# Half of a shared expert moved from the router's stage into the opening of the attention, in a one-core Flamingo stack

## The reference

```
x = x + tanh(g_xattn[0]) * quantised_expert(layernorm(x), ...)        # layer 1
x = x + tanh(g_ffn[0])   * ffn0(layernorm(x))                         # layer 2
x = x + tanh(g_xattn[1]) * attention(layernorm(x), ctx, pos)          # layer 3
x = x + tanh(g_ffn[1])   * ffn1(layernorm(x))                         # layer 4
```

```
scores = softmax(xt @ gate_w.T);  idx = top_k(scores + gate_b, 2)
y = sum over the 2 chosen experts of weight * (silu(xt @ W1[e].T) * (xt @ W3[e].T)) @ W2[e].T
z = (silu(xt @ Ws1.T) * (xt @ Ws3.T)) @ Ws2.T                         # shared expert, every token
return y + z
```

## Time and profile before

| | us |
|---|---|
| median of three runs | 1374.13 |
| the profiled execution | 1370.09 |
| its span | 1368.3 |
| TensorE busy | 1163.8 (85%) |
| VectorE busy | 826.9 (60%) |
| ScalarE busy | 672.5 (49%) |
| GpSimd busy | 404.8 (30%) |

### The profile page before, as it was taken

One profiled execution on the slowest core, in us unless ns is written; L12 is line 12 of the kernel. 1 busy time (PEld: TensorE's weight loads), 2 busy tenths in 40 slices (PEclk: granted clock), 3 DMA queues, 4 the chain that ended last, 5 costly groups with the idle time before them and its releaser, 6 DMA issues.

```text
span 1368.3 us, 16555 instructions
## 1 busy us (share of the span) xinstructions
PE 1163.8 (85%) x5247; PEld 510.3 (37%) x5309; DVE 826.9 (60%) x1275; ACT 672.5 (49%) x1191; POOL 404.8 (30%) x477
## 2 busy tenths in 40 slices
PE   5787786999699999953459989999999999888898
PEld 3454444555344444421013222222332222234443
DVE  6787855116055555215788888777877777613543
ACT  3565564545222222242347666566656556763453
POOL 5555720111222222113434432222222233102332
PEclk9998998999899999985669999999999999999999
DMA  7333135432434444337713332222222236200011
GB/s 253 116 108 108 58 120 182 162 127 92 158 123 147 150 144 147 100 129 216 192 51 106 90 103 73 81 86 79 71 88 78 83 84 67 37 1 8 32 39 47
DMA packets 110452, 141.58 MB, mean 103 GB/s; under 512 B 24888, under 2 KB 79672, under 8 KB 110376
## 3 DMA queue, kind: packets, MB, share of 16 engines
q1 hardware_dynamic: 91528, 111.37, 25.3%
q0 software_dynamic: 18368, 28.85, 8.3%
q10 hardware_dynamic: 480, 0.39, 0.1%
HBM read 97.44 MB, written 46.27 MB: 105 GB/s over the span
## 4 chain that ended last, share of the span: by engine, by line
PE 30%; DVE 9%; issue 8%; ACT 6%; POOL 2%; DMA 1%; POOLq 0%; ACTq 0%; DVEq 0%
PE PS L2717 8%; PE PS L2687 5%; PE PS L2631 5%; PE PS L2655 5%; ACT a_E L2798 4%; PE PS L2704 4%; DVE a_top L2975 4%; POOL a_K L2029 1%; DMA a_attnT<-f_y,l_pos 1%; PE PS L2258 1%; DVE a_tab L2055 1%; DVE a_early L2877 1%; PE PS L2281 1%; PE PS L2627 1%; PE PS L2648 0%
## 5 line engine op out<-in xcount | busy, mean ns | idle before, releaser
L2975 DVE TENSOR_REDUCE a_top<-PS 128x2 f32<-128x1024 f32 x256 | 308.3, 1222 | 94.1 <-PE PS L2704 89.9
L2798 ACT ACTIVATE a_E<-PS 128x512 f32<-128x512 f32 x512 | 277.7, 596 | 147.7 <-PE PS L2687 147.4
L2687 PE MATMUL PS<-a_Q,a_K 99*128 99x512 bf16 (+1 forms) x468 | 157.4, 387 | 17.5 <-ACT a_E L2798 7.6
L2704 PE MATMUL PS<-a_K,a_Q 64*128 64x512 bf16 x512 | 104.5, 405 | 45.9 <-DVE a_top L2975 26.9
L1464 PE MATMUL PS<-f_W,f_GT 128*128 x312 | 141.9, 598 | 0.0
L2717 PE MATMUL PS<-a_E,a_V 128*32 128x512 f32 x1024 | 139.0, 615 | 0.6 <-ACT a_E L2798 0.4
L2687 PEld LDWEIGHTS PS<-a_Q,a_K 99*128 99x128 bf16 (+1 forms) x512 | 44.4, 97 | 154.2 <-ACT a_E L2798 102.3
L1891 POOL TENSOR_TENSOR a_qf<-a_qf,a_tab 128x512 f32<-128x512 f32 x15 | 19.1, 1271 | 267.1 <-DVE a_swapped L2899 267.1
L1520 DVE TENSOR_TENSOR f_H<-f_SG,PS 128x256 f32<-128x256 f32 x39 | 16.4, 421 | 125.1 <-ACT f_SG L1504 125.1
L1464 PEld LDWEIGHTS PS<-f_W,f_GT 128*128 128x128 f32 x312 | 57.0, 193 | 57.4 <-issue 57.4
L2704 PEld LDWEIGHTS PS<-a_K,a_Q 64*128 64x128 bf16 x512 | 24.7, 93 | 139.2 <-issue 73.5
(11 more groups left out here) (362 smaller groups left out, 1987.7 us busy)
## 6 DMA issues: line engine op xcount, KB each, us to landing
f0r_raw<-in_L_ffn_W_dram SPq DMA_DIRECT2D x24, 512.0 KB, 4.9
a_K<-k_parts SPq DMA_DIRECT2D x192, 64.0 KB, 2.3
a_Q<-a_q_parts SPq DMA_DIRECT2D x186, 64.0 KB, 2.5
f_y<-f_Y SPq DMA_DIRECT2D x39, 256.0 KB, 2.0
v_units<-V SPq DMA_DIRECT2D x16, 512.0 KB, 2.9
a_V<-v_units SPq DMA_DIRECT2D x16, 512.0 KB, 3.6
k_parts<-f_k_parts SPq DMA_DIRECT2D x16, 384.0 KB, 3.5
a_q_parts<-a_parts SPq DMA_DIRECT2D x16, 384.0 KB, 2.7
```

The source lines that it names most:

```text
L2687: nc.tensor.matmul(PS[:, 4 + h % 2, :], K6[k][0:rows_, o, head // 2, kt * P:(kt + 1) * P], Q6[k][0:rows_, o, head // 2, :], start=True, st ...
L2704: last = nc.tensor.matmul(PS[:, 2 * pair + o, :], Q6[k][at, o, h // 2, t * P:(t + 1) * P], K6[k][at, o, h // 2, :], start=True, stop=True)
L2798: nc.scalar.activation(E[step % 2][:, h, :], PS[:, 4 + h % 2, :], ACT.Exp).then_inc(exp_done, 1)
L2975: nc.vector.tensor_reduce(top[:, h - h % 2:h - h % 2 + 2, t], PS[:, 2 * pair:2 * pair + 2, :], AX.X, ALU.max).then_inc(maxed, 1)
```

## The change

1. **The front runs the shared expert for eight tiles, not sixteen.** The batches are taken in the order 2, 0, 3, 1. For batches 0 and 1 the shared expert is computed as before, one tile with one expert's six fills (four behind the up product, two behind the transposes of H). Batches 2 and 3 only go through the router; ScalarE's queue stores their transposed rows to DRAM. The shared weights stay in SBUF, in a buffer that later serves as the exponentials' `E0` and as `attn`.
2. **The other eight tiles run in the attention's opening** (`LateTiles`). Two loads of 1 MB bring the transposed rows into `attnT0` and into `wo`; the first is SP's first transfer, the second takes the place of Wout's load, which waits for the last up product. VectorE makes the gate product and adds the result straight from PSUM. A table `LATE` says which step stands in which slot.
3. Rows of tiles 8 to 15 are added in turns (0, 0) to (0, 3), two tiles to a turn; the `fill`s of the constant rows stand at slots of a table; ScalarE's half of the first queries' load goes from the end of turn (-1, 1) to slot 3 of (-1, 2).
4. **In the last stage** batch 2 is normalised and batch 3's statistics are taken beside the last projections, in turn (4, 0); `choose` is cut in two around the second gate product.

```
         def front(first_set, turn, logit, tile, choose, count, place):
             turn(0)
             logit(0)
+            first_set()
+            turn(1)
+            tile(0, lambda: logit(1), None)
+            tile(1, None, None)
+            turn(2)
+            tile(2, lambda: logit(2), None)
+            turn(3)
...
+            tile(3, last_logits, None)
+            tile(4, None, count)
+            tile(5, None, None)
+            tile(6, None, place)
+            tile(7, None, None)
...
             def turn(n):                      # ScalarE
...
+                if TURNS[n] in LATE:
+                    act.wait_ge(xT_ready, (n + 1) * DC)
+                    act.dma_start(xT_late[TURNS[n] - LATE[0]], xT[BUFFER[n]][:]).then_inc(xT_stored, 16)
...
+            def tile(j, beside, behind):      # TensorE
+                for c in range(DC):
+                    last = nc.tensor.matmul(PS[:, 5, 0:2 * I], rows[:, c, at], shared13[:, c, :], start=(c == 0), stop=(c == DC - 1))
+                last.then_inc(up_done, 1)
+                if beside:
+                    beside()
+                for f in fills(j)[:DC]:
                     turned.tensor(pe, f)
+                if behind:
+                    behind()
                 if j:
                     down(j - 1)
                 pe.wait_ge(gated, j + 1)
...
                 last.then_inc(h_turned, 1)
+                for f in fills(j)[DC:]:
+                    turned.tensor(pe, f)
...
+class LateTiles:
+    DOWN = (6, 0, 1, 2, 6, 6, 6, 6)
...
+    def load(self, sp, k):
+        sp.dma_start(self.homes[k], self.xT_dram[k]).then_inc(self.loaded[k], 16)
+    def silu(self, act, n):
+        act.wait_ge(self.up_done, n + 1)
+        if n >= 2:
+            act.wait_ge(self.gated, n - 1)
+        self.nc.scalar.activation(self.SG[n % 2], self.bank(n)[:, 0:self.I], ACT.Silu).then_inc(self.silu_ready, 1)
+    def gate(self, v, n):
+        v.wait_ge(self.silu_ready, n + 1)
...
+        self.nc.vector.tensor_tensor(self.H[n % 2], self.SG[n % 2], self.bank(n)[:, self.I:2 * self.I], ALU.mult).then_inc(self.gated, 1)
+    def add(self, v, n):
+        v.wait_ge(self.down_done, n + 1)
+        x = self.X[:, self.first + n, :]
+        self.nc.vector.scalar_tensor_tensor(x, self.PS[:, self.DOWN[n], :], self.tgate, x, ALU.mult, ALU.add).then_inc(self.added, 1)
...
+        LATE = {(-1, 0): {9: [("g", 2, 0), ("y", 0, 0), ("y", 1, 0), ("t", 2, 0)]},
+                (-1, 2): {4: downs(2) + ups(3), 5: [("g", 3, 0), ("y", 2, 0)] + ups(4), 6: [("t", 3, 0), ("g", 4, 0)] + downs(3),
...
         def tiles_to_add(b, c):
-            if b == -1:
-                return [TB + 2 * c, TB + 2 * c + 1]
-            if b == 0:
-                return [3 * TB + c]
+            if b == -1 and c < 2 or b == 0:
+                first = TB + 2 * c if b == -1 else 2 * TB + 2 * c
+                return [first, first + 1]
             return []
...
                 def scores(unit, step, h):
-                    if not (is_first(unit) and step == 0 and h < 2):
+                    if is_first(unit) and step == 0 and h < 2:
+                        pe.wait_ge(late.HT_ready, late.N)
...
+            FILLS = {(-1, 0): {11: [(1, 0)], 12: [(1, 1)], 13: [(1, 2)]}, (-1, 1): {4: [(1, 3)]},
+                     (-1, 2): {3: [(2, 0), (2, 1)], 8: [(2, 2)], 9: [(2, 3)], 10: [(3, 0)], 11: [(3, 1)], 12: [(3, 2)], 14: [(3, 3)]}}
...
+                if b == NB:                   # VectorE
+                    def third_rows():
+                        v.wait_ge(x_added, 3 * TB)
+                        f1.statistics(v, 2)
...
+                    at(6, third_rows)
+                    at(8, third_normalized)
+                    for t in range(TB - 1):
+                        at(10 + 2 * t, lambda t=t: fourth_rows(t))
```

More of the change, by code:

```diff
@@ L815, in moe_front @@
-        LAST = NB - 1
-        def front(first_set, turn, logit, tile, choose, count, place, end):
+        shared13, shared2 = shared_weights(shared_w, I, D)
+        turned = Weights(nc, sb, sem, PS, identf, W13, W2, shared13, shared2, *raw)
+        SG = [sb(f"SG{k}", [P, I]) for k in range(2)]
+        UP = [sb(f"UP{k}", [P, I]) for k in range(2)]
+        H = [sb(f"H{k}", [P, I]) for k in range(2)]
+        HT = [sb(f"HT{k}", [P, IC, P]) for k in range(2)]
+        Z = [sb(f"Z{k}", [P, D]) for k in range(TB)]
@@ new lines, in moe_front, with fills, fills_in_front, front @@
+        up_done, silu_ready, gated, h_turned = sem("up_done"), sem("silu_ready"), sem("gated"), sem("h_turned")
+        HT_ready, down_done, z_ready, added = sem("HT_ready"), sem("down_done"), sem("z_ready"), sem("added")
+        FILLS = Weights.FILLS
+        assert E == NS
+        def fills(j):
+            return range(FILLS * (j + 1), FILLS * (j + 2))
+        def fills_in_front(n):
+            return FILLS * (0, 1, 3, 4)[n]
+        def front(first_set, turn, logit, tile, choose, count, place):
@@ L2698, in maxima @@
                             pe.wait_ge(ones_ready, 4 * (k + 1))
-                    if not (is_first(unit) and h == 0):
+                    if is_first(unit) and h == 0:
+                        pe.wait_ge(late.added, 3 + pair)
+                    else:
                         pe.wait_ge(maxed, n_max(unit, h, pair) - 2)
@@ L2836, in _, with add_rows @@
             rows.vector_start(v)
-            for t in range(TB):
+            rows.vector(v, 0)
+            late.gate(v, 0)
+            rows.vector(v, 1)
+            late.gate(v, 1)
+            rows.vector(v, 2)
+            rows.vector(v, 3)
+            def add_rows(t):
+                if t >= late.first:
+                    v.wait_ge(late.added, t - late.first + 1)
                 rows.vector(v, t)
@@ L2946, in outs @@
                                                            ALU.mult, ALU.add).then_inc(x_added, 1)
+                    for kind, m, part in late_jobs(b, c, n):
+                        if kind == "g":
+                            late.gate(v, m)
+                        if kind == "y":
+                            late.add(v, m)
                 if (b, c) == (NB - 1, 2):
```

480 lines of the change are left out of this document (290 added, 190 removed).

## The result

The changed kernel takes 1333.62 us (median of 4 runs, 1332.65 to 1335.91) against 1372.93 (4 runs) of the kernel before: a ratio of 0.9708, with a 95% interval of 0.9691 to 0.9725. In two later comparisons it was 0.9698 (0.9679 to 0.9717) and 0.9714 (0.9695 to 0.9733). 1328.5 was forecast, 1318 to 1346 as range. The profiled execution took 1335.91 us, the longest of the first four, with a span of 1334.1 us: 34.2 less than before, where the medians differ by 39.3.

What follows compares the result with a forecast made beforehand. TensorE bounds the front and leads the body; gathers, a chain and VectorE bound the opening in turn. -39 + 1.5 + 3 - 8.5 = -43.0 from 1370.09 gives 1327.1, plus 1.4 for the median: 1328.5, range 1318 to 1346.

Steps and rivals of the forecast that it cites:

- The front, -39: Front of layer 2: eight tiles less give 43.0 us, less 1.6 and 2 of waits; -39, between -43 and -34.
- the bound of 3.0: Front, tile 1: largest wait for raw W1/W3, landing after at most 9.2 us and needed after 6.2.
- The second rival: Front becomes bound by raw weight loads: seven tiles wait 3.0 us each, +19, 1347 us; chance 0.08.
- To the first transposes, +1.5: Opening's start: 1 MB more at the head of SP's queue delays the gathers; +1.5 us.
- The strict reading, +3.9: Opening's start: the added 1 MB load ahead of the gathers is paid in full, +3.9 us instead of +1.5.
- Clock and queries, -1.5: Opening: late tiles keep the clock up; transposes gain, queries' gain is lost to fills on ScalarE; -1.5 us (0 to -3).
- The queries' load, +2: Opening: ScalarE's half is issued later, behind second unit's queries and two fills; tiles 3 and 4 included; +2 us (0 to +4).
- The maxima, -1.5: Opening, VectorE-bound: four row pairs leave (-6.0), gates and adds come (+3.5), +1 for TensorE-led slots; -1.5 us (-2.5 to +12).
- First unit +1, body +3: First unit: down product, add and Exp table at its head, +1 (0 to +4). Body: four more waits behind adds, +3.
- The last stage, -8.5: Last stage: earlier statistics shorten two waits for xT and keep the clock; -8.5 us, between -11 and -5.
- The third rival: Opening gets shorter: gathers lose nothing, VectorE's gain comes through, clock stays up; -6 instead of +1.5, 1321 us; chance 0.10.
- The first rival: Opening can't take the tiles: clock stays low in the maxima; +18 instead of +1.5, 1345 us; chance 0.15.

Runs made afterwards that it cites:

- the four edits: Changed kernel with third store later, first units' K and V loads behind the gathers, third silu behind square root, batch 1's normalising behind seventh gate: 1319.8 us, 0.9619.

## Why the prediction was right, step by step

- **The front, -39: held,** -37.5 in the profile. Eight tiles less is as reckoned, the turns wait 0.97 us each instead of 0.8, and the router costs nothing. The mis-sized term is tile 1's load, 2 forecast, 3.42 of waiting and 1.5 of low clock measured (in the other profiles mostly 2.6 and 1.4). The store was named as what disturbs it, and moving it gives 3.6 us of the front back. But the bound of 3.0 had a mistake in it. It counted 6.2 us from request to need, with a down product of 1.7 us between. Tile 0 has no tile before it and so no down product: the loads are issued at 248.28 and needed at 252.77, 4.5 us later. They land after 7.9, inside the 9.2 of the earlier trace rows, from which the bound should have been 4.7, with the fall of the clock on top. The second rival (every tile late) did not come: tiles 2 to 7 wait for no weights.
- **To the first transposes, +1.5: right within the scatter,** and not shown closer than that: +1.2, +1.2, +1.4, +1.6, +2.7, +3.6 and +4.2 in seven profiles, against a single one of before. The strict reading, +3.9 for the megabyte ahead, falls: the same megabyte once more cost 0 and 1.2 us. What the gathers pay for is the K and V loads beside them (with the second half of the turned rows behind these), and K and V stood there before the change too. That queues share the DMA engines, as the Trainium skill says (Trainium Kernel Development and Optimization, Key Constraints), agrees with the 4 us that leave with those loads; it doesn't give the price of a load ahead.
- **Clock and queries, -1.5: wrong.** Transposes still at 1.11 and queries of 5.9 to 6.6 us (5.38 before) made it +0.5 to +1.2. The forecast had the late tiles shortly ahead of them; they end 5 to 8 us earlier, and the clock falls in between. Where they end 0.8 us earlier, it holds (0.66 and 3.67).
- **The queries' load, +2, and tiles 3 and 4:** with the item above the stretch from transposes to maxima grew by 0.4 to 1.1 (forecast +0.5).
- **The maxima, -1.5: the step that failed,** +3.2 to +4.7. Three things are in it. First, the forecast took four row pairs off this stretch (6 us), but only three stood in it; in the kernel before, the fourth is added behind TensorE's first scores (704.26):
```profile
704.71 0.74 DVE L1577 SCALAR_TENSOR_TENSOR X<-a_rows,a_tw,X 128x512 f32<-128x512 f32 x1
```
Three pairs are 4.5 us, and without late tiles the stretch is 3.2 shorter (42.0 to 38.8). Second, of the tiles' price 6.5 was measured instead of 4.5. VectorE's busy time went from 41.0 to 41.6 us, where three pairs less and 3.5 us of late tiles more would be 40.0, and its idle time grew from 1.1 to 3.7 us. Third, and part of that, late tiles have a fixed order against VectorE's other work: the seventh gate stands behind a normalising of 2.28 us, and TensorE waits 3.47 us for it. The move behind the gate brings the maxima to 44.0 and 43.5 us, so 1.3 us or more hang on it; what the rest is, no run shows.
- **First unit +1, body +3: less than forecast,** -0.2 and +1.2, and undoing the move won nothing in the body. VectorE's idle time takes most of the extra adds: nearer to the lower bound of 0 than to the 0.75 us behind each.
- **The last stage, -8.5: held.** It lasts 110.4 us where before had 120.7, and undone it costs 9.9. Of the 10.3 us, 1.6 are the last down product (3.53 before, 1.90 here), which comes at either level of the clock from profile to profile; 8.7 stay.
- The sum was 5.1 us short of the measured median, inside the forecast's own range. That is in part luck. The opening without the first unit grew by 5.4 to 8.6 us instead of 0.5, and the last projections, which the forecast put at nothing, by 2.4; the first unit and the body came out 3 us better than forecast and the last stage 1.8, which hides about half of it. The third rival (a shorter opening) did not come as the change was written; with the four edits the opening is 4 us shorter than before. The first rival had the sign of the opening right and its cause wrong: the clock in the maxima was 0.92. (Its three terms add up to 19.9, not 18.)

What stays open: the last unit's projections. They took 14.0 us before and in three variants, 16.3 to 17.0 us in ten other profiles of the changed kernel and its variants. TensorE waits three times shortly ahead of them, 0.80, 0.90 and 0.77 us before and in the kernel without late tiles, which both came out fast. In the other twelve the middle wait is 1.04 us, and of these two were fast. Whether the change made this likelier can't be said from one profile of before, and nothing was tried on it.

## What to carry to other kernels

When work is moved into another stage's gaps, list for each piece what stands in front of it on every engine: two waits here were one short instruction queued behind something unrelated (a gate behind a normalising, a square root behind a silu), and both went away by a change of order. Reckon each piece's time from request to need by its own neighbours, the first of a series above all: it has nothing of a predecessor in front of it. And check on the timeline that work counted as leaving a stretch stood in it. A load that comes within a few us of its need should be priced with the store that starts beside it, and with the clock's fall behind the wait (fills of 1.94 us took 3.39 behind 3.42 us of waiting). One profile is one draw: the same stretch of the same kernel differed by 3 us between profiles, as much as the terms that were argued over.

## What the runs showed that was not expected

- The same amount of traffic costs very differently: a 1 MB store 1.2 us ahead of two needed loads of 0.5 MB each cost 3.6 us, a 1 MB load ahead of indirect gathers put the fourth rows off by 0 to 1.2 us, and 26 loads of K and V (64 KB mostly, 2.6 MB in all) with 1 MB behind them, beside the gathers, 4 us or more. Size of the transfers and place in time change together in these, so which of the two counts isn't shown.
- The time from the program's start to the front's first turn, in code that no variant touches, was 225.2 to 229.2 us in the profiles.
- TensorE's clock level at a given place is not a property of the kernel alone: the last projections came out at 14.0 or at 16.3 to 17.0 us, the last down product at 1.9 or 3.4 to 3.6. Also among profiles with the same waits ahead (0.80, 1.04 and 0.77 us, and 1.10 us) both levels occur.
